# Second attention: the slot read with the exponentials as the stationary operand, two heads side by side, turned back by TensorE

## The reference, cut to what matters

```python
q, k, v = ...                      # (heads, 256, 128), q and k rotated
s   = clip(hs @ Ws1.T @ Ws2.T + bs2, -32, 32)        # (heads, 256, 64)
z   = cumlogsumexp(s, axis=2)                        # over the tokens
es  = exp(s)
enz = exp(-z)
A   = where(mask, q @ k.T * scale, 0)
ok  = enz * (A @ es)               # the slots are read: (heads, 256, 64)
qv  = softmax(ok)
W2  = where(mask, (qv * enz) @ es.T, 0)              # the slots are written
o   = W2 @ v
out = (rms_norm(o) * g * sigmoid(g)) @ Wo.T
```

## Time and profile before

| | us |
|---|---|
| median of 3 runs (1990.83 to 1996.87) | 1991.45 |
| the profiled execution | 1976.93 |
| its span, from the first to the last instruction | 1974.3 |
| TensorE busy, whole span | 1862.6 (94%) |
| VectorE busy | 1272.3 (64%) |
| ScalarE busy | 906.5 (46%) |
| GpSimd busy | 829.3 (42%) |
| second attention, by L1302 (first start) and L1347 of the last pair | 670.4 to about 1672 |

### The profile page before, as it was taken

How to read it: one execution, slowest core, us unless ns; L and a number is a source line. 1 busy time by engine, 2 the same in 40 slices (tenths; PEclk the granted TensorE clock), 3 DMA queues, 4 the chain that set the end, 5 groups by cost and what they waited for, 6 DMA issues and landing times.

```text
span 1974.3 us, 34673 instructions
## 1 busy us (share of the span) xinstructions
PE 1862.6 (94%) x11822; PEld 1472.1 (75%) x11822; DVE 1272.3 (64%) x2811; ACT 906.5 (46%) x2978; POOL 829.3 (42%) x919
## 2 busy tenths in 40 slices
PE   6999999999988799899999999999999998999986
PEld 4667676766766677788888888888888886777754
DVE  5677777773456586776676666666766664444467
ACT  3646465553433343345445444554554553444422
POOL 2000000330046455466766676767677664000066
PEclk9999999999999798899999999999999998999999
DMA  9600000114342000000000000000000122433344
GB/s 337 224 1 1 1 2 1 46 52 129 100 160 68 32 1 11 1 9 17 14 16 16 8 21 11 21 8 12 20 11 19 55 95 94 124 107 105 107 124 130
DMA packets 75896, 114.15 MB, mean 58 GB/s; under 512 B 9504, under 2 KB 65952, under 8 KB 73088
## 3 DMA queue, kind: packets, MB, share of 16 engines
q1 hardware_dynamic: 66416, 86.38, 13.3%
q0 software_dynamic: 9216, 25.18, 3.9%
q10 hardware_dynamic: 144, 1.05, 0.1%
HBM read 64.86 MB, written 47.71 MB: 57 GB/s over the span
## 4 chain that ended last, share of the span: by engine, by line
PE 79%; DVE 9%; POOL 5%; issue 2%; DMA 2%; ACT 2%; POOLq 0%; DVEq 0%; SPq 0%; ACTq 0%
PE ps L1261 11%; PE ps L1276 9%; PE ps L1347 6%; PE ps L1712 5%; PE ps L598 4%; PE ps L1302 4%; PE ps L582 3%; PE ps L617 3%; PE ps L1290 3%; PE ps L1289 3%; PE ps L1288 2%; PE ps L861 2%; PE ps L1283 2%; POOL work L1907 2%; PE ps L588 2%
## 5 line engine op out<-in xcount | busy, mean ns | idle before, releaser
L1261 PE MATMUL ps<-work,weights 128*128 128x256 f32 x1024 | 249.8, 387 | 4.7 <-DVE work L1498 4.7
L1276 PE MATMUL ps<-split 128*128 128x512 f32 x768 | 233.1, 426 | 1.5 <-DVE split L1515 1.5
L1261 PEld LDWEIGHTS ps<-work,weights 128*128 128x128 f32 x1024 | 187.2, 192 | 27.3 <-DVE work L1498 6.2
L1605 POOL TENSOR_TENSOR work<-work,rope 128x512 f32<-128x512 f32 x128 | 164.5, 1285 | 62.9 <-ACT work L1436 62.9
L460 POOL DMA_INDIRECT xg<-work x96 | 97.7, 1018 | 164.5 <-PE ps L588 152.8
L1611 POOL TENSOR_TENSOR work<-work 128x512 f32<-128x512 f32 x128 | 162.9, 1273 | 5.1
L701 ACT ACTIVATE work<-ps,work 128x128 f32<-128x128 f32 x256 | 95.4, 373 | 147.2 <-DVE work L800 145.2
L1907 POOL DMA_INDIRECT work<-yg,work x64 | 62.3, 974 | 227.2 <-DMA yg<-work 207.6
L1276 PEld LDWEIGHTS ps<-split 128*128 128x128 f32 x768 | 133.9, 194 | 27.7 <-issue 1.8
L739 DVE COPY work<-ps 128x384 f32<-128x384 f32 x256 | 129.6, 547 | 9.0 <-PE ps L598 8.9
L1520 DVE TENSOR_TENSOR work<-ps,keep_w 128x384 f32<-128x384 f32 x128 | 65.4, 552 | 108.1 <-PE ps L1284 108.1
(11 more groups left out here) (230 smaller groups left out, 4596.8 us busy)
## 6 DMA issues: line engine op xcount, KB each, us to landing
work<-xg SPq DMA_DIRECT2D x118, 128.0 KB, 2.2
yg<-work SPq DMA_DIRECT2D x118, 128.0 KB, 1.7
xg<-work SPq DMA_DIRECT2D x6, 2048.0 KB, 16.7
weights<-in_w SPq DMA_DIRECT2D x8, 1024.0 KB, 9.3
weights<-in_f SPq DMA_DIRECT2D x8, 1024.0 KB, 5.1
weights<-in_f SPq DMA_DIRECT2D x1, 4864.0 KB, 17.5
work<-xn SPq DMA_DIRECT2D x32, 128.0 KB, 2.2
weights<-in_wo SPq DMA_DIRECT2D x1, 2048.0 KB, 9.0
```

The costliest lines, as they stand in the source:

```text
L1261: last = pe.matmul(ps[:, 2, which * SEQ:(which + 1) * SEQ], w1(h, (which * KC + kc) * P, P), xT[:, kc, :], start=kc == 0, stop=kc == KC - 1)
L1276: last = pe.matmul(ps[:, 3, :], x1_split[:, xp, kc, c * P:(c + 1) * P], w_vg[:, n % 2, wp, kc, :], start=i == 0, stop=i == KC * len(TERMS) ...
L1605: pool.tensor_tensor(qk[:, h % 4, :, :], raw[:, h % 2, :, :], rope[:, 0, :].unsqueeze(1).broadcast_to([P, 2, SEQ]), ALU.mult).then_inc(rot ...
```

## The change

`slots_read` swaps its operands. The exponentials of a head (`es`, 128 keys x 64 slots) become the stationary operand, and the masked scores `aT` the moving one, 128 columns at a time. The first head of the pair uses columns 0 to 63 of the array and writes partitions 0 to 63 of PSUM, the second columns 64 to 127 and partitions 64 to 127. The six matmuls alternate between the two heads. The outcome has the slots on the partitions, so it is turned back: ScalarE copies it to SBUF (`okT`), TensorE turns it with two transposes into bank 1 (`turn_ok`), and VectorE multiplies it by `enz`, now in one instruction over both heads. The transposes stand behind the first three of the six matmuls of `values_gates`. `turn_og`, which writes bank 1 too, gets a wait for that multiplication. A signal that nobody waited for (`v1_ready`) goes, and one load's semaphore is shared with an earlier one.

```diff
+        okT = carve("slots", ST, P)
...
                 for hh in range(2):
                     h = 2 * pp + hh
                     pe.wait_ge(aT_ready.sem, aT_ready.at(t, h + 1))
-                    last = over_keys([ps[:, 4 + hh, BLK + c * M:BLK + (c + 1) * M] for c in range(ST)], aT[:, hh, :],
-                                     [es[:, pp % 2, c, hh * M:(hh + 1) * M] for c in range(ST)])
+                for tile, j, at in ((0, 0, 0), (1, 0, P), (1, 1, SEQ)):
+                    for hh in range(2):
+                        a = slice(M * hh, M * hh + M)
+                        last = pe.matmul(ps[a, 4 + tile, BLK:BLK + P], es[:, pp % 2, j, a], aT[:, hh, at:at + P],
+                                         start=j == 0, stop=j == tile, skip_group_check=True)
                 last.then_inc(ok_done.sem, 1)
+
+            def turn_ok(pp):
+                pe.wait_ge(okT_ready.sem, okT_ready.at(t, pp + 1))
+                for c in range(ST):
+                    last = pe.transpose(ps[:, 1, c * P:(c + 1) * P], okT[:, c, :], ident[:, :])
+                last.then_inc(ok_turned.sem, 1)
...
                 if now:
                     slots_read(pp)
                 if ahead:
-                    values_gates(pp + 1, 0)
+                    values_gates(pp + 1, 0, range(0, 3))
+                if now:
+                    turn_ok(pp)
+                if ahead:
+                    values_gates(pp + 1, 0, range(3, 6))
                 if behind:
...
+                    if now:
+                        pe.wait_ge(ok_step.sem, ok_step.at(t, 2 * pp + 1))
                     turn_og(pp - 1)
...
                     exp_scores(pp + 1)
                     copy_qk(2 * pp + 2)
+                if now:
+                    act.wait_ge(ok_done.sem, ok_done.at(t, pp + 1))
+                    act.copy(okT, ps[:, 4:6, BLK:BLK + P]).then_inc(okT_ready.sem, 1)
                 if further:
                     upper_vg(pp + 2)
...
-                    dve.wait_ge(ok_done.sem, ok_done.at(t, pp + 1))
-                    for hh in range(2):
-                        last = dve.tensor_tensor(okz[:, :, hh, :], ps[:, 4 + hh, BLK:512].rearrange("p (c m) -> p c m", c=ST),
-                                                 enz[:, pp % 2, :, hh * M:(hh + 1) * M], ALU.mult)
-                    last.then_inc(ok_step.sem, 1)
+                    dve.wait_ge(ok_turned.sem, ok_turned.at(t, pp + 1))
+                    dve.tensor_tensor(okz.rearrange("p c h m -> p c (h m)"), ps[:, 1, 0:SEQ].rearrange("p (c n) -> p c n", c=ST),
+                                      enz[:, pp % 2, :, :], ALU.mult).then_inc(ok_step.sem, 1)
```

More of the change, by code:

```diff
@@ L1181, in build @@
         qk_done, vg_done, a_done, ok_done = count("qk_done", NH1), count("vg_done", NH1), count("a_done", NH1), count("ok_done", PAIR1)
+        okT_ready, ok_turned = count("okT_ready", PAIR1), count("ok_turned", PAIR1)
         qe_turned, w2_done, o_done = count("qe_turned", PAIR1), count("w2_done", NH1), count("o_done", NH1)
@@ L1185, in build @@
         s1_upper, es_ready = count("s1_upper", 1), count("es_ready", PAIR1)
-        raw_ready, v1_ready, gate_tanh = count("raw_ready", NH1), count("v1_ready", NH1), count("gate_tanh", NH1)
+        raw_ready, gate_tanh = count("raw_ready", NH1), count("gate_tanh", NH1)
         okp_ready, qeT_ready, ssq_ready = count("okp_ready", PAIR1), count("qeT_ready", PAIR1), count("ssq_ready", NH1)
@@ L1441, in gates @@
                 a = 2 * (n % 2)
-                act.copy(v1[:, a:a + 2, c, :], vg[:, :, 0, :]).then_inc(v1_ready.sem, 1)
+                act.copy(v1[:, a:a + 2, c, :], vg[:, :, 0, :])
                 if n >= 2 and c == 0:
@@ L1690, in build @@
             again(n, TILES) for n in (z_ready, out_th_ready, z_gated, z_mixed, x1_ready))
-        h4_cleared, z4_step, sh1_loaded = again(h_cleared, 1), again(z_step, 0), sem("sh1_loaded")
+        h4_cleared, z4_step, sh1_loaded = again(h_cleared, 1), again(z_step, 0), again(f0_loaded, 32)
         def pe_blocks1(pe):
@@ L1770, in pe_blocks1 @@
             turn_h(NB1 - 1, 2)
-            pe.wait_ge(sh1_loaded, 16)
+            pe.wait_ge(sh1_loaded.sem, sh1_loaded.at(0, 16))
             for c in range(TILES):
@@ L2018, in _ @@
             slots_over(sp)
-            sp.dma_start(shared1, A["sh1"]).then_inc(sh1_loaded, 16)
+            sp.dma_start(shared1, A["sh1"]).then_inc(sh1_loaded.sem, 16)
             for b in range(NB1):
```

## The result

| | before | after |
|---|---|---|
| median of 4 runs, us | 1994.16 (1990.83 to 1997.69) | 2021.44 (2014.37 to 2024.53) |
| ratio, 95% interval | | 1.0132 [1.0097, 1.0166] |
| profiled execution, us | 1976.93 | 2021.55 |
| L1302 (L1304 after), first to last start, us | 670.4 to 1654.6 | 672.7 to 1684.1 |
| span behind that, us | 319.7 | 335.6 |

The change makes the kernel 1.3% slower; 2021.1 us was forecast. The second attention is 1011.4 - 984.2 = 27.2 us longer.

The account below looks back on a forecast made before the run. Settled pairs were taken as bound by TensorE and VectorE's rotation, tied. The rotation coming 0.54 us later gave 25.9 + 2.9 + 0.8 = 29.6 us, so 1991.45 + 29.6 = 2021.1 us, range 2009 to 2035.

Parts of the forecast that it names:

- The bound: Settled pairs of the second attention: VectorE's rotation and TensorE tied; a rotation later by x stretches the pair by x.
- TensorE's own work: TensorE's read, first values and gates, and transposes in a pair: -1.28 + 0.78 + 0.16 + 0.22 = -0.12 us.
- The swap with its dearer first values and gates: TensorE's read falls from 1.28 to 0.78 us; the values and gates behind it cost 0.16 more.
- The path: From read through ScalarE's copy, transposes and multiplication to VectorE's rotation: odd head's load starts 0.54 us later a settled pair.
- The sum: Delay over all 64 pairs of the second attention: 25.9 + 2.9 + 0.8 = 29.6 us.
- the term of 28.8 us: 48 settled pairs at 0.54 us (25.9) and 7 at a sequence's end at 0.42 us (2.9).
- First sequence: Its 8 pairs: four where VectorE sits behind GpSimd, 0.2 us each, 0.8 in all; four where TensorE comes late, 0.
- TensorE alone: Rival: VectorE's rotation has hidden slack, so the pair shortens by 0.12 us, 1984 us in all; chance 0.05.
- A looser tie: Rival: slack near 0.5 us before the odd head's load, or the gain used up exactly, 1991 us; chance 0.04.
- The copy's wait: Rival: transposes wait for ScalarE's copy, 0.2 us more a settled pair, +12, 2033 us; chance 0.15.
- Heads side by side: Forecast: the read's two heads run side by side; rival: they do not, +0.66 us a pair, +36, 2057 us; chance 0.04.
- The clock: Rival: TensorE's clock falls as it stands 0.65 us a pair; for a third of pairs more than +100; chance 0.02.

Follow-up runs that it names:

- Rotation first: Changed kernel with VectorE rotating the even head before it takes up the read slots: 1962.29 us against 1979.31 before, ratio 0.9931.
- the spare multiplication: Kernel before plus one VectorE multiplication of 128x256 whose outcome nobody reads: 1992.44 us against 1979.31, ratio 1.0083.
- the two traces of before: Kernel before, unedited, traced twice: first profiled execution 1976.93 us; once more on the second chip, 1988.36 us in one run.
- the swap alone: Changed kernel without ScalarE's copy, the two transposes and the added wait, outcome not the reference's: 1968.28 us, ratio to the kernel before 0.9960.
- the first experiment: Changed kernel with VectorE rotating the even head before it takes up the read slots: 1962.29 us, ratio to the kernel before 0.9931.

## Why the prediction was right

- **The bound.** The step that carried it was to see, under a 99.8% busy TensorE, that L1498 and L1261 were tied at 0.05 us. Rotation first removes the loss with all the added work in place, and the spare multiplication brings a loss with nothing else changed. Shown: TensorE's own pace before was 14.87 us a pair, so the tie had 0.03 us to give.
- **TensorE's own work** was put at -0.12 us a pair; against TensorE's own pace of 14.87, rotation first shows 14.80, so -0.07. The swap with its dearer first values and gates gave -0.33 where -0.34 was forecast; turning back cost 0.26 where 0.22, the price of two transposes, was forecast.
- **The path.** +0.54 us forecast, +0.57 measured: 0.03 more from the read (0.81 for 0.78), 0.01 each from the transposes and the chain on VectorE (1.94 us for 1.93), and 0.02 less between the transposes' end and VectorE's start (0.02 for 0.04).
- **The sum.** 29.6 us forecast; the attention grew by 27.2 against one trace of before and 31.4 against the other. The medians moved by 27.3. From the ninth pair on, where the term of 28.8 us lies (25.9 + 2.9), it grew by 30.7 or 29.4; the first sequence came out 3.4 us shorter than in the first trace of before and 2.1 longer than in the second. So the sum is closer than its terms: a settled pair lost a little more than forecast, and the first sequence, which varies by itself, covered it. The forecast 2021.1 stands on a before of 1991.45, which has become 1994.16 with a fourth run, so that its last decimals are luck.
- **First sequence.** The price of 0.2 us a pair can't be checked: the two traces of before differ there by more than the whole term. That GpSimd holds VectorE's difference there was right; that this floor lies also just under the settled pairs was not seen, and cost the expectation of the swap alone.
- **The rivals.** TensorE alone: would have been right with the rotation moved, which is the kernel of the first experiment. A looser tie: there were 0.03 us, not 0.5. The copy's wait: it stayed hidden by less than 0.1 us. Heads side by side: held. Their order is worth 0.26 us a pair; the 0.66 that the rival priced, for no overlap at all, no run shows. The clock: its full level held in the settled pairs. Its price was worked out wrongly: a third of 55 pairs of 15.4 us at 0.83 of the clock is 15.4 x 55 / 3 x (1 / 0.83 - 1), some 58 us and not more than 100.

## What to carry to other kernels

Where an instruction of a fully busy engine starts 0.05 us behind the signal that it needs, and 0.05 us is what a signal costs in that trace, two paths are tied, though no idle time shows it: compare ends and starts before pricing a change by the busy engine's work alone. If swapping the operands leaves the outcome in another layout, count what it passes through to be turned back, and put other work of the waiting engine (here a rotation) into that gap in the same edit. When one wait is removed, look for the next one just under it.

## What the runs showed of the hardware

- Entering a divided array (64 columns each) cost about 0.15 us by an estimate from the chain (12 records in 0.81, where six steps of 0.11 are 0.66), leaving it about 0.2 (0.89 against 0.70 for three matmuls).
- Two heads in different columns ran side by side when their matmuls alternated (0.81 us for the read), and overlapped in part when they came one head after the other (1.07).
- A VectorE `tensor_tensor` of 128x256 with both inputs in SBUF took 0.54 to 1.47 us instead of 0.42 where a GpSimd `tensor_tensor` had started before it, ending 0.28 us behind that one in all 56 such pairs of the swap alone. The multiplication and the reduction next to it, with one input in SBUF, kept their 0.42 meanwhile.
